# Feed-forward edge products of three blocks in one run, and late rows moved from VectorE to GpSimd

## The reference

```
h  = act_quant(layernorm(x)) @ weight_quant(w1).T        # 256 -> 1024
h  = depthwise_conv1d(h, taps of 3 tokens, padding 1)     # along the tokens
u  = silu(h)
out = x + act_quant(u) @ weight_quant(w2).T               # 1024 -> 256
```

## Time and profile before

| what | value |
|---|---|
| median of 3 runs | 439.9 us (439.56 to 439.93) |
| profiled execution, first to last instruction (span) | 436.6 us |
| profiled execution, own time | not recorded apart from its span; the median lies 3.3 us above the span |
| mean granted clock of TensorE | 0.996 |
| busy: PE, DVE, ACT, POOL | 93%, 86%, 72%, 20% |

### The profile page before, as it was taken

The page is one execution under the profiler, slowest core; times in us unless marked ns, Lnnn a source line. Parts: engine busy times, 40 slices in busy tenths (PEclk is TensorE's granted clock), DMA queues, the critical chain, the costliest instruction groups (busy, mean ns, idle before and its releaser), DMA issues.

```text
span 436.6 us, 13819 instructions
## 1 busy us (share of the span) xinstructions
PE 406.0 (93%) x5914; PEld 275.4 (63%) x5914; DVE 377.0 (86%) x598; ACT 313.9 (72%) x367; POOL 86.1 (20%) x115
## 2 busy tenths in 40 slices
PE   1999997799999999999999999999999988899985
PEld 1666675566666666666666666666676644576664
DVE  4789987987887889789879879889879899999994
ACT  2456767589979756757666766767666589999984
POOL 2175554850000120020120020111001010221200
PEclk9999999999999999999999999999999998999999
DMA  7802000612111111111211111111101000001002
GB/s 215 226 2 72 2 2 1 227 44 74 50 40 63 38 39 62 51 38 47 67 38 39 62 39 51 62 39 41 49 33 44 3 0 0 2 26 48 26 26 80
DMA packets 27588, 22.53 MB, mean 52 GB/s; under 512 B 7232, under 2 KB 27268, under 8 KB 27524
## 3 DMA queue, kind: packets, MB, share of 16 engines
q1 hardware_dynamic: 26112, 21.59, 15.2%
q10 hardware_dynamic: 1412, 0.01, 0.2%
HBM read 6.91 MB, written 2.10 MB: 21 GB/s over the span
## 4 chain that ended last, share of the span: by engine, by line
PE 56%; DVE 25%; ACT 12%; issue 3%; DMA 2%; ACTq 0%; DVEq 0%; POOL 0%
PE sc L1691 14%; DVE arena L722 14%; PE heads L1708 7%; PE heads L1709 5%; PE heads L1710 5%; PE heads L1517 4%; ACT arena L1290 3%; PE sc L1528 3%; ACT qq L1379 3%; PE by L1596 2%; ACT qq L1387 2%; PE bx L1528 2%; PE by L1528 2%; PE sc L1795 2%; DMA lng<-in_L_xattn_ln_x_b 2%
## 5 line engine op out<-in xcount | busy, mean ns | idle before, releaser
L722 DVE SCALAR_TENSOR_TENSOR arena<-arena 128x1024 bf16<-128x1024 f32 x160 | 194.0, 1243 | 30.2 <-ACT arena L1290 29.1
L1290 ACT ACTIVATE arena<-sc,kb 128x1024 f32<-128x1024 f32 x160 | 169.9, 1115 | 67.6 <-PE sc L1691 67.5
L1708 PEld LDWEIGHTS heads<-v,arena 128*128 128x128 bf16 x1280 | 117.1, 97 | 39.2 <-issue 28.3
L1708 PE MATMUL heads<-v,arena 128*128 128x65 f16 x1280 | 130.2, 194 | 3.8 <-DVE arena L722 3.5
L1709 PE MATMUL heads<-v,arena 128*128 128x64 f16 x1280 | 129.3, 195 | 0.0
L1710 PE MATMUL heads<-v,arena 128*128 128x65 f16 x1280 | 128.7, 192 | 0.0
L1691 PE MATMUL sc<-qs,kst 64*128 64x512 f16 x960 | 118.0, 378 | 2.2 <-DVE kk L664 1.5
L1709 PEld LDWEIGHTS heads<-v,arena 128*128 128x128 bf16 x1280 | 118.8, 97 | 0.1
L1710 PEld LDWEIGHTS heads<-v,arena 128*128 128x128 bf16 x1280 | 118.8, 99 | 0.0
L1691 PEld LDWEIGHTS sc<-qs,kst 64*128 64x128 f16 x960 | 40.0, 94 | 48.1 <-issue 5.0
L519 POOL TENSOR_SCALAR frs<-fmv 128x2 f32<-128x2 f32 x8 | 7.9, 990 | 150.9 <-DVE fmv L790 150.9
(11 more groups left out here) (215 smaller groups left out, 586.4 us busy)
## 6 DMA issues: line engine op xcount, KB each, us to landing
kst<-kk SPq DMA_DIRECT2D x80, 128.0 KB, 2.0
xs<-in_x SPq DMA_DIRECT2D x8, 256.0 KB, 5.4
qs<-qq SPq DMA_DIRECT2D x16, 128.0 KB, 2.0
out<-cbuf SPq DMA_DIRECT2D x7, 256.0 KB, 2.1
xs<-in_ctx SPq DMA_DIRECT2D x6, 256.0 KB, 5.3
xs<-in_L_ffn_w SPq DMA_DIRECT2D x1, 1024.0 KB, 6.8
cbuf<-in_L_ffn_w SPq DMA_DIRECT2D x1, 1024.0 KB, 8.8
arena<-in_L_xattn_W_kv SPq DMA_DIRECT2D x2, 256.0 KB, 5.0
```

Source lines behind the costliest of these rows:

```text
L722: e.scalar_tensor_tensor(out=rest[:, j, :, :], in0=prob[:, j, :, :], scalar=SHRINK, in1=probh[:, j, :, :], op0=ALU.mult, op1=ALU.subtract) ...
L1290: a_.activation(prob[:, j, :, :], sc[(j + 1) % 2][:, :, :], ACT.Exp, bias=kb[:, bass.ds(i * QUAD + j, 1)]).then_inc(exp_done[j], 1)
L1708: t_.matmul(o, hi, row[:, 0:OW], start=first and sub == 0, stop=False, skip_group_check=True)
```

## The change

- The late rows' last three steps (scaled back, high, low) leave DVE. POOL gets them as `late_rows(i)`, behind the two inverse roots and ahead of all scales of the tiles; the steps are chained by a new semaphore `late_back`.
- PE no longer multiplies the edges of blocks 1, 2 and 3 one after the other, two columns each. `hidden_edges(False)` does all three at once, six columns in each of the 32 matmuls, into bank 5. It waits for all eight row blocks in `xd`. `edges` grows to hold a column pair for each block, and DVE makes one product of 48 numbers in place of three of 16.
- PE's order becomes hidden(1, 2), late rows 0, hidden(1, 3), late rows 1, tokens_first(0, 0), hidden(1, 4), the edges of blocks 1 to 3, tokens_first(0, 1).
- ACT's order becomes silu(0, 2), center(1, 1), silu(0, 3), center(1, 2), rows_t of late rows 0, center(1, 3), rows_t of late rows 1, center(1, 4), quantize(0, 0).

```
+            def late_rows(i):
+
+                pool.wait_ge(late_rounded[i], 1)
+                for t in range(2):
+                    c = 2 * i + t
+                    last = g.tensor_scalar(y_late[i][:, t, :], y_late[i][:, t, :], ROUND, fq[:, 1, c:c + 1], ALU.subtract, ALU.mult)
+                last.then_inc(late_back[i], 1)
+                pool.wait_ge(late_back[i], 1)
+                g.tensor_copy(dq_late[i][:, 0, :, :], y_late[i]).then_inc(late_back[i], 1)
+                pool.wait_ge(late_back[i], 2)
+                g.tensor_tensor(dq_late[i][:, 1, :, :], y_late[i], dq_late[i][:, 0, :, :], ALU.subtract).then_inc(s["dq_ready"], 1)
+
             for i in range(2):
                 prep_scale(NB - 2 + i, slice(2 * i, 2 * i + 2))
+            for i in range(2):
+                late_rows(i)
...
+            def edge_products(first):
+
+                ns = slice(0, 1) if first else slice(1, NF)
+                count_ = 1 if first else NF - 1
+                dve.wait_ge(s["edge_ps"], 1 if first else 2)
+                taps = cw[:, :, 0:3:2].rearrange("p j (n e) -> p j n e", n=1).to_broadcast([P, J, count_, 2])
+                e.tensor_tensor(edges[:, :, ns, :], edge_bank(first), taps, ALU.mult).then_inc(s["edge_step"], 1)
...
                 late_scale(1)
-                late_scaled_back(0)
                 late_inverted(1)
-                late_high(0)
                 edge_taps(0, 2)
-                late_low(0)
                 left_tap(0, 7)
-                late_scaled_back(1)
                 right_tap(0, 7)
-                late_high(1)
                 edge_taps(0, 3)
-                late_low(1)
...
                     largest(n - 1, 0)
-                    edge_products(n)
+                    if n == 1:
+                        edge_products(False)
...
                 center(1, 1)
+                silu(0, 3)
+                center(1, 2)
                 rows_t(NB - 2)
-                silu(0, 3)
-                rows_t(NB - 1)
-                center(1, 2)
                 for n in range(1, NF):
                     center_ahead(n, 3)
+                    if n == 1:
+                        rows_t(NB - 1)
...
-                pe.wait_ge(s["xd_ready"], min(NB, 2 * n + 3) if n else NB - 2)
-                if n == 1:
+                pe.wait_ge(s["xd_ready"], NB - 2 if first else NB)
+                if not first:
                     pe.wait_ge(s["x1_ready"], NB)
-                elif n > 1:
-                    pe.wait_ge(s["uf_ready"], (n - 1) * FT)
...
-                if t == 1 and n < NF - 1:
-                    pe.wait_ge(s["edge_step"], n + 2)
+                if m == 1:
+                    pe.wait_ge(s["edge_step"], 2)
...
                 hidden(1, 1)
+                hidden(1, 2)
                 late_rows_first(0)
-                hidden(1, 2)
-                hidden_edges(1)
-                late_rows_first(1)
                 for n in range(1, NF):
+                    if n == 1:
+                        hidden(1, 3)
+                        late_rows_first(1)
                     tokens_first(n - 1, 0)
-                    hidden_ahead(n, 3)
                     if n > 1:
+                        hidden_ahead(n, 3)
                         hidden_first(n - 2, 3)
-                    if n > 1:
-                        hidden_edges(n)
                     hidden_ahead(n, 4)
+                    if n == 1:
+                        hidden_edges(False)
                     tokens_first(n - 1, 1)
```

More of the change, by code:

```diff
@@ L161, in xattn_ffn @@
         fu = sb("fu", [P, 4, FT], F32)
-        edges = sb("edges", [P, J, 2], F32)
+        edges = sb("edges", [P, J, NF, 2], F32)
         shifts = sb("shifts", [P, 4], F32)
@@ L247, in xattn_ffn @@
         late_rounded = [sem(f"late_rounded{i}") for i in range(2)]
+        late_back = [sem(f"late_back{i}") for i in range(2)]
         stored = [sem(f"stored{i}") for i in range(2)]
@@ L263, in xattn_ffn, with edge_bank, edge_columns @@
         ob = [bank[7][:, 0:D], bank[6][:, 0:D]]
-        def edge_bank(n):
-            b = bank[7][:, D:D + 2 * J] if n == 0 else bank[5][:, 0:2 * J]
-            return b.rearrange("p (j e) -> p j e", e=2)
+        def edge_bank(first):
+            if first:
+                return bank[7][:, D:D + 2 * J].rearrange("p (j n e) -> p j n e", n=1, e=2)
+            return bank[5][:, 0:2 * J * (NF - 1)].rearrange("p (j n e) -> p j n e", n=NF - 1, e=2)
+        def edge_columns(k, w, first):
+            at_ = xd[:, k, w, 0:1] if first else xd[:, k, w, FB:FB + 1]
+            return bass.AP(at_.tensor, at_.offset, [at_.ap[0], (FB, 1 if first else NF - 1), (FB + 1, 2)])
         def product_bank(n, t):
@@ L920, in right_tap @@
                                        op0=ALU.mult, op1=ALU.add).then_inc(s["taps_done"], 1)
-            def edge_products(n):
-                dve.wait_ge(s["edge_ps"], n + 1)
-                e.tensor_tensor(edges[:, :, :], edge_bank(n), cw[:, :, 0:3:2], ALU.mult).then_inc(s["edge_step"], 1)
+            def edge_products(first):
[4 more added lines that the diff above has]
+                e.tensor_tensor(edges[:, :, ns, :], edge_bank(first), taps, ALU.mult).then_inc(s["edge_step"], 1)
             def edge_taps(n, k):
                 js = slice(2 * k, 2 * k + 2)
-                dve.wait_ge(s["edge_step"], n + 1)
+                dve.wait_ge(s["edge_step"], 1 if n == 0 else 2)
                 dve.wait_ge(s["taps_done"], n * J + 2 * k + 2)
                 c = ct[n % 3][:, js, 0:FB:FB - 1]
-                e.tensor_tensor(c, c, edges[:, js, :], ALU.add).then_inc(s["edge_done"], 1)
+                e.tensor_tensor(c, c, edges[:, js, n, :], ALU.add).then_inc(s["edge_done"], 1)
             def largest(n, t):
@@ L977, in late_inverted @@
                 e.reciprocal(fq[:, 2, 2 * i:2 * i + 2], fq[:, 1, 2 * i:2 * i + 2]).then_inc(late_inverse[i], 1)
[L979 to L992, removed]
             def feed_forward():
@@ L1816, in hidden_edges @@
                         for w in range(2):
-                            last = t_.matmul(edge_bank(n)[:, j, :], w1t[:, k, j * P:(j + 1) * P], xd[:, k, w, n * FB:n * FB + FB + 2:FB + 1],
+                            last = t_.matmul(edge_bank(first)[:, j, :, :], w1t[:, k, j * P:(j + 1) * P], edge_columns(k, w, first),
                                              start=(q == 0), stop=(q == 3))
@@ L1886, in feed_forward @@
                 hidden(0, 2)
[L1887 removed]
+                hidden_edges(True)
                 hidden(0, 3)
```

4 lines of the change are left out of this document (2 added, 2 removed).

## The result

| | before | after |
|---|---|---|
| median, 6 runs each | 439.91 us (438.59 to 440.33) | 442.35 us (441.32 to 444.07) |
| ratio, with 95% interval | | 1.0061 (1.0034 to 1.0087) |
| span of the profiled execution | 436.6 us | 442.2 us |

The change made the kernel slower by 2.4 us. Timed once more (12 executions against 32), the ratio was 1.0043 (1.0024 to 1.0063). The six executions spread by 1.7 us before and by 2.8 us after, and the profiled one after is the slowest of its six, 444.07 us; so the two spans alone (5.6 us apart) overstate the loss. One execution of the kernel before, timed beside the first experiments, took 664.55 us at a mean granted clock of 0.564; no ratio counts it.

A forecast was written before the change was run, and what follows sets the result against it. DVE was taken to bound the passage from block 0 to 1, ACT and DVE the steady run. Passage +0.5, steady run -0.1: span 436.6 to 437.0, median 439.9 to 440.3 us; 8-in-10 range 439.1 to 441.4.

The forecast's parts named there:

- T: POOL's time for one late row block: bounds 2.0 to 5.6 us, taken as 2.8, hidden up to 3.0.
- S: Start of PE's tokens_first(0, 0): forecast 368.55, set by ACT, against 367.92 before; POOL alone would allow 368.1.
- POOL becomes the bound: Rival: T over 3.0 makes POOL set S; at T = 3.6 the time is 441.4 us. Chance 15%.
- R: Start of late_rounding(0) on ACT, last point the change doesn't touch: 360.79 before, where the prediction's walk begins.
- ACT's list and the wait of tokens_first for its copy: ACT's queue from 360.79 ends late rows 0's rows_t at 368.4; tokens_first waits for that bank, 0.6 us later than before.
- The relation of the train to the edge product: ACT/PE chain from quantize(0, 0) on, paced by DVE's block 1 work: as if started at S + 3.65, 0.5 us later.
- The 32 merged matmuls: PE's six-column edge products, costed like two-column ones; upper bound 0.9 us more, nothing added.
- The rival of the falling clock: Rival: PE, waiting about 1.2 us for late rows 1, drops to 1.2 GHz; 2.6 us more, up to 443. Chance 5%.
- POOL held up by two edge taps: Shared-port rule: two DVE edge taps of 0.16 us could delay POOL by 0.3 us in all; forecast would stand.
- The median above the span: Whole kernel: the median was taken to run 3.3 us above the profiled span.
- 3 us of freed DVE time: Rival that ACT closes up the passage: quantize(0, 0) at 370.6, 1.1 us earlier, time 438.7 us. Chance beyond 0.2%: 12%.

The follow-up runs named there:

- the first experiments: The earliest follow-up kernels, timed beside the kernel before; the text does not list which ones. The first described kept the late rows' scaling on DVE: ratio 1.0035.
- Pool only: Kernel before with only the late rows' three steps moved to POOL, edges and orders as before: 443.25 us, ratio 1.0070.
- no hold: Changed kernel with scaling back on DVE, that of late rows 1 behind edge_taps(0, 3); cast and subtraction on POOL: 439.10 us, ratio 0.9982.
- scale on DVE: Changed kernel with the late rows' scaling back returned to DVE, cast and subtraction left on POOL: 440.62 us, ratio 1.0035.
- order only: Changed kernel with all three late-row steps back on DVE; merged edges and new PE and ACT orders stay: 440.91 us, ratio 1.0025.
- the filler: Changed kernel with eleven extra 512-column matmuls on PE, ahead of the transposes of late rows 1, into an unread bank: 442.58 us, ratio 1.0055.
- pool bench: Kernel before with six extra POOL instructions into unused memory, between attention and late rows, to measure their prices: one execution, 440.31 us.
- own bank: Kernel before with late rows on POOL, transposed into the second product's bank behind the first tokens, ACT's second copy behind whole(0, 0): 440.49 us, ratio 1.0017.
- edges sooner: As no hold, but PE does the merged edges ahead of hidden(1, 4): 439.59 us, ratio 0.9993.
- best: Kernel before with cast and subtraction on POOL, late rows 0 transposed into a free bank, late rows 1 behind tokens_first(0, 0): ratio 0.9980, again 0.9968.

## Why the prediction was wrong

**The step that failed** is the price of POOL's new work, T: the term of two tensor_scalar of 256 columns, taken as 0.4 us each. They measure 1.15. I had bounds of 0.3 and 1.6 from the earlier trace rows and took a value by the low one. The upper row, three of L548 in 4.80 us, I read as three short instructions held up by DVE, because the small L519 changes from 1.25 to 0.21 with DVE's load. POOL's prices (1.17 us with nothing to hold it up) make it likely that most of those 1.6 us were the instruction's own. T became 4.2 and not 2.8, past the 3.0 at which POOL sets S. The rival "POOL becomes the bound", at 15%, is what happened. By its own formula S = 361.97 + 2 x 4.2 + 0.5 = 370.9, 2.3 later than I had, and 440.3 + 2.3 = 442.6 against 442.35 measured and 441.18 in the repetition, so that the close fit to the first is partly luck (in the profile S is 10.50 behind R, or 371.3 on the time axis of before, as the transposes ahead of it ran at the lower clock). Pool only, with the same R to S as the changed kernel, and no hold, where POOL is off the path, show this cause from both sides, and their intervals are far apart (1.0051 to 1.0089, 0.9964 to 1.0000). The predicted range reached to T = 3.6 though the sum's own upper bound was 5.6.

**What was right.** ACT's list and the wait of tokens_first for its copy: 7.70 for 7.76, once POOL was hidden. The relation of the train to the edge product: it should start as if at E + 0.76, with E the left tap behind DVE's edge product. In the profile after E is 0.13 us ahead of quantize(0, 0), which gives 0.63 us added behind it; 0.68 was measured. For scale on DVE it gives 0.33, and 0.32 was measured; for order only 0.86, and 0.94. In no hold it gives 0.33 where 0.05 was measured, so it is good to some 0.3 us. The 32 merged matmuls took no longer than those of two columns, as taken (1.00 us for 0.99).

**The clock.** The rival of the falling clock, at 5%, was real as well, but as part of POOL's. Behind the 2.69 us of waiting, PE's transposes, tokens_first and hidden(1, 4) took 0.82, 1.71 and 1.20 us in place of 0.44, 0.88 and 0.87: 1.5 us in this execution. In the repetition, executions of the changed kernel lie at 440.6 to 441.7 us in nine cases and at 443.3 to 443.8 in three. That the three are those in which the clock fell there is likely, not shown; the filler did not settle it. The kernel before has such a stretch too (0.83 from 360 to 370 us), but in its profile at 362.1 to 365.5, where PE had time; in pool bench's it lay over tokens_first.

**The Trainium skill's rule of the shared port** ("SBUF — State Buffer", "Who interferes with whom") held for POOL's subtraction, with the other side as the loser. I had weighed it as POOL held up by two edge taps for 0.3 us. In scale on DVE it was DVE's edge tap that was held by POOL, for 1.0 us, on ACT's path. In own bank an edge tap took 0.55 us, in no hold, edges sooner and best 0.25 to 0.26: each ended with POOL's subtraction. But the rule names any POOL instruction that reads SBUF, and for the scalings the traces do not agree. In the changed kernel POOL's pair of scalings ran from 363.14 to 365.45, and the edge taps beside them took 0.30 and 0.17 us:

```profile
363.33 0.30 DVE L957 TENSOR_TENSOR kk<-kk,edges 128x4 f32<-128x4 f32 x1
```

**The median above the span.** I had added 3.3 us, from the median of some runs and the span of another. Run by run the difference is 2.1 to 2.2 us for the kernel before and 1.8 to 1.9 for all others but pool bench, which is 2.1. The forecast should have added some 0.3 us less. Why it differs is not shown.

**Not settled.** Why no hold is faster than the walk says: R to the end is 75.99 us against 75.81 before in the profiles, and the median is 1.0 us lower. 0.3 of it is the difference just named; the rest lies within the spread of the kernel before, whose executions gather at spans of about 436.0 and 437.8 us. What makes these two groups is not shown. The profiles of before and of pool bench lie 1.6 us apart in span, 0.74 of it ahead of R and 0.86 behind it.

## What to carry to other kernels

Moving work to an idle engine pays only if the moved chain, at that engine's prices, ends before the engine that is next in line; here ACT stood right behind DVE, so that, by the prediction's estimate, 3 us of freed DVE time could give 1.1 at most, and POOL's 8.4 us in their place were not hidden. Where the trace has only loaded examples of the operation, keep the loaded price in the range, or time the form by itself, as six spare instructions did here. To take a step off a path, look first at what it must wait for: a free PSUM bank for the transposes and the split of the work by price (scaling on DVE, cast and subtraction on POOL) gave 0.2 to 0.3%, where moving all of it lost 0.4 to 0.6%. Before two profiles are compared to a microsecond, see where in each the clock is low and how each execution lies in the spread of its kernel.

## What the runs showed of the hardware

- POOL's tensor_scalar on f32 costs 1.17 us for 256 columns and 0.74 for 128, against 0.61 for a cast of 512, 0.75 for a product of two tiles of 256 and 1.16 for one of 512. DVE takes 0.35 for the same scaling of 256 columns.
- A DVE instruction of four columns with two SBUF inputs took 1.17 us beside a POOL subtraction of 1.15; with a PSUM and an SBUF input, 0.74 us as ever. Beside POOL's scalings the same four columns took 0.30 and 0.17 us, alone 0.16.
- 32 matmuls of 6 columns take 0.99 to 1.01 us, those of 2 columns 0.99.
- The clock fell at the end of PE's wait of 2.69 us, and the transposes, tokens_first and hidden(1, 4) behind it took 1.5 us more for it.
- A stretch at the lower clock stands in all 14 profiles between 361 and 375 us, at different places; over tokens_first(0, 0) it makes 0.88 us into 1.46 to 1.74.
